# A four-layer graph network kernel: layer 3's linear score term moves from two TensorE products a block to one GpSimd add

## What is computed

```
hp = h @ lin_w.T + lin_b
u = hp @ W1.T;  v = hp @ W2.T
s = u[:, :, None, :] + v[:, None, :, :]
s = where(s > 0, s, 0.2 * s)
e = einsum('bijf,f->bij', s, a[:, 0])
e = where(adj > 0, e, -9e15)
out = elu(softmax(e) @ hp)
```

## Time and profile before

| | |
|---|---|
| median of 3 runs | 8483.6 us (8482.73 to 8487.48) |
| the profiled execution | 8497.64 us, span 8495.8 us |
| PE, DVE, ACT, POOL busy | 92%, 88%, 87%, 18% |
| mean granted clock of PE | 0.981 |
| one pass in the middle | 520 us |
| chain of work that ended last | PE 53%, DVE 16%, issue 14%, ACT 13% |

### The profile page before, as it was taken

One profiled execution on the slowest core, in us unless ns is written; L12 is line 12 of the kernel. 1 busy time (PEld: TensorE's weight loads), 2 busy tenths in 40 slices (PEclk: granted clock), 3 DMA queues, 4 the chain that ended last, 5 costly groups with the idle time before them and its releaser, 6 DMA issues.

```text
span 8495.8 us, 175156 instructions
## 1 busy us (share of the span) xinstructions
PE 7806.9 (92%) x64968; PEld 3570.9 (42%) x64968; DVE 7445.0 (88%) x10867; ACT 7388.3 (87%) x8641; POOL 1519.0 (18%) x582
## 2 busy tenths in 40 slices
PE   4889999899999999989899999999989999899998
PEld 2535344353443534435353443534435344353442
DVE  4789898898988989889898888988889898898888
ACT  3699888898888898889888888988889888898888
POOL 1212121121211112121121211212112121111000
PEclk8999999999999999999999999999999999999999
DMA  3626254362543625335253452624426254362430
GB/s 81 166 56 148 65 122 96 75 151 56 123 93 84 142 61 125 89 84 131 60 136 78 98 119 59 146 68 114 104 65 150 62 122 96 78 150 56 107 72 20
DMA packets 501426, 830.78 MB, mean 98 GB/s; under 512 B 89890, under 2 KB 155426, under 8 KB 500514
## 3 DMA queue, kind: packets, MB, share of 16 engines
q1 hardware_dynamic: 500514, 818.85, 41.5%
HBM read 76.25 MB, written 4.19 MB: 9 GB/s over the span
## 4 chain that ended last, share of the span: by engine, by line
PE 53%; DVE 16%; issue 14%; ACT 13%; SPq 2%; DMA 2%; DVEq 0%; ACTq 0%; POOL 0%; POOLq 0%
PE psum L871 23%; PE psum L784 9%; PE psum L746 7%; DVE work L1472 7%; ACT work L1130 6%; PE psum L742 4%; ACT work L994 4%; ACT work L985 3%; PE psum L765 2%; PE psum L677 2%; DVE work L1280 2%; DVE work L1308 2%; SPq L549 2%; DMA work<-work 1%; PE psum L672 1%
## 5 line engine op out<-in xcount | busy, mean ns | idle before, releaser
L1130 ACT ACTIVATE work<-v,ucol 128x1024 f32<-128x1024 f32 x3727 | 4021.4, 1141 | 318.8 <-PE psum L871 317.2
L871 PE MATMUL psum<-work,pick 128*32 128x512 f32 x32768 | 3919.9, 605 | 294.9 <-DVE top L1423 132.1
L1472 DVE TENSOR_SCALAR work<-v,ucol 128x1024 f32<-128x1024 f32 x4465 | 3379.1, 809 | 293.2 <-PE psum L871 265.7
L871 PEld LDWEIGHTS psum<-work,pick 128*32 128x32 f32 x32768 | 930.8, 110 | 2520.2 <-issue 1983.3
L1280 DVE CUSTOM_DVE_ANT_0 work<-psum,work 128x1024 f32<-128x1024 f32 x1280 | 1538.0, 1202 | 324.2 <-ACT work L985 304.4
L1308 DVE STREAM_TRANSPOSE work<-work 128x1024 f32<-128x1024 f32 x1280 | 1583.8, 1237 | 70.6 <-DMA work<-work 68.6
L994 ACT ACTIVATE work<-work,least 128x1024 f32<-128x1024 f32 x1280 | 1464.2, 1144 | 4.5 <-DVE least L1280 4.4
L985 ACT ACTIVATE work<-psum,beta 128x1024 f32<-128x1024 f32 x1024 | 1139.0, 1112 | 325.8 <-PE psum L746 267.4
L784 PEld LDWEIGHTS psum<-work,vw 128*64 128x64 f32 x16384 | 878.3, 137 | 613.8 <-issue 605.1
L784 PE MATMUL psum<-work,vw 128*64 128x128 f32 x16384 | 1119.7, 279 | 8.0 <-DMA work<-work 8.0
L742 PE MATMUL psum<-mask,ident_b 128*128 128x512 bf16 x2560 | 780.1, 387 | 236.8 <-DVE least L1280 181.5
(11 more groups left out here) (159 smaller groups left out, 5010.0 us busy)
## 6 DMA issues: line engine op xcount, KB each, us to landing
work<-work SPq DMA_DIRECT2D x2560, 256.0 KB, 4.6
adj_in<-in_adj SPq DMA_DIRECT2D x128, 512.0 KB, 4.6
tile3T<-blocks SPq DMA_DIRECT2D x512, 128.0 KB, 2.7
x_in<-in_x SPq DMA_DIRECT2D x16, 256.0 KB, 4.6
xT_both<-in_xT SPq DMA_DIRECT2D x16, 256.0 KB, 5.3
out<-yout SPq DMA_DIRECT2D x16, 256.0 KB, 2.6
work<-in_WqT SPq DMA_DIRECT2D x1, 128.0 KB
work<-in_WkT SPq DMA_DIRECT2D x1, 128.0 KB
```

Source lines behind the costliest of these rows:

```text
L871: mm = pe.matmul(score3[32 * q:32 * q + 32, cols], pick[:, 15 - kk:47 - kk], ring[u % RING][q][:, cols], start=(kk == 0), stop=(kk == 15), ...
L1130: ins = act.activation(ring[u % RING][q], v3[:], ACT.Relu, bias=ucol[:, 4 * T + q, kk:kk + 1])
L1472: ins = dve.tensor_scalar(ring[u % RING][q], v3[:], ucol[:, 4 * T + q, kk:kk + 1], 0.0, ALU.add, ALU.max)
```

## The change

The linear part is kept in `column3` in plain fp32. ACT's copy at slot 3 stays, but rounds nothing and frees the PSUM pair itself; DVE's subtraction at slot 4 is gone, and so are PE's two products in each block. Instead GpSimd writes, once a block, `column3` plus the block's mask tile into `probs3` (`mask_tile3`), and DVE's closing reduction reads `probs3` in place of the bf16 mask tile. GpSimd may do so once the block before has been transposed out of `probs3` (semaphore `s_blocks3`), that is from step 5 on; the call stands at step 6. A new semaphore, `s_mask3`, tells DVE that the sum is there; ACT waits for it too before it overwrites `column3` in the next pass.

For this GpSimd's program is rewritten to walk the slots as the other engines' do, with the conversions at slots of their own (`CONVERT_AT`) and the head adds three slots after their heads (`ADD_AT`). `convert` 4 now comes before `add_pair` 0. In slot order the new add stands: block 0 at slot 6, 1 at 22, 2 at 38, 3 at 54, 4 at 74, 5 at 102, 6 at 132, 7 at 150 (just after the deviation at slot 149 and before `convert` 6 at 152). The costs in `side_work` are changed to match, so that the split of ring units is computed anew.

```diff
-        column3 = sb("column3", [P, N], F32R)
+        column3 = sb("column3", [P, N])
...
-                if kk == (3 if T else 12):
-                    if T == 0:
-                        pe.wait_ge(freed(it3[0], ("column3", 0)), uses_before(it3[0], ("column3", 0)) + 1)
-                    for c in range(2):
-                        cols = slice(c * HALF, (c + 1) * HALF)
-                        pe.matmul(score3[:, cols], row0[:], column3[:, cols], start=False, stop=False,
-                                  skip_group_check=True)
...
-            def column_3(it):
+            def column_3(g, it):
+                if not_first(g):
+                    act.wait_ge(s_mask3, g * NT)
                 filled(act, it, ("column3", 0))
-                act.activation(column3[:], place(it, ("column3", 0)), ACT.Copy).then_inc(s_column3_hi, 1)
+                act.activation(column3[:], place(it, ("column3", 0)), ACT.Copy).then_inc(freed(it, ("column3", 0)), 1)
...
-            def top_tile3(g, T, mask):
+            def top_tile3(g, T):
                 ready(s_ring_free, ONE + g * GROUPS + (T + 1) * 16)
-                dve.tensor_tensor_reduce(probs3[:], score3, mask[:, T, :], -1.0, 3.0e38, ALU.add, ALU.min,
+                ready(s_mask3, g * NT + T + 1)
+                dve.tensor_tensor_reduce(probs3[:], score3, probs3[:], -1.0, 3.0e38, ALU.add, ALU.min,
                                          top3[:]).then_inc(s_top3, 1)
...
-            def column_3(g, it):
-                dve.wait_ge(s_column3_hi, g + 1)
-                low = column3[F:P, :]
-                dve.tensor_tensor(low, place(it, ("column3", 0))[F:P, :], low.bitcast(F32), ALU.subtract)\
-                   .then_inc(freed(it, ("column3", 0)), 1)
...
+            def mask_tile3(g, T, it):
+                if T or not_first(g):
+                    ready(s_blocks3, g * NT + T)
+                if T == 0:
+                    in_sbuf(pool, it, ("column3", 0))
+                pool.tensor_tensor(probs3[:], column3[:], mask_ring(it)[:, T, :], ALU.add).then_inc(s_mask3, 1)
...
+CONVERT_AT = {66: 0, 71: 1, 77: 2, 83: 3, 95: 4, STEPS.index(96) + 2: 5, 152: 6}
+ADD_AT = {s + 3: p for s, p in HEADS_AT.items() if p < HP - 1}
```

More of the change, by code:

```diff
@@ L235, in side_work @@
         dve += 1.25 if kk == 5 else 0.0
-        pe += {3: 0.8, 13: 1.1}.get(kk, 0.0)
+        pe += {13: 1.1}.get(kk, 0.0)
     dve += 1.4 if s in TOP3_AT else 0.0
@@ L432, in build @@
         s_q_hi = sem("s_q_hi")
-        s_column3_hi = sem("s_column3_hi")
+        s_mask3 = sem("s_mask3")
         s_relu = sem("s_relu")
@@ L1141, in layer3 @@
                     if s == 3:
[L1142 removed]
+                        column_3(g, it)
                     if kk is not None and STEPS[s] + 1 < GROUPS:
@@ L1473, in ring_units, with last_top @@
                 ins.then_inc(s_ring_dve, 1)
-            def last_top(g, it, s, tail):
+            def last_top(g, s, tail):
                 T = TOP3_AT.get(s)
                 if T:
-                    top_tile3(g, T - 1, mask_ring(it))
+                    top_tile3(g, T - 1)
                 elif T == 0 and tail:
-                    top_tile3(g - 1, NT - 1, mask_ahead(it))
+                    top_tile3(g - 1, NT - 1)
             def slots(g, it, tail, a, flagged, at):
@@ L1488, in slots @@
                         first_of(a, it, s)
-                    if g is not None and s == 4:
-                        column_3(g, it)
                     if g is not None and kk is not None:
@@ L1551, in _ @@
             layer3(B - 1, last, True, False)
-            top_tile3(B - 1, NT - 1, mask_ring(last))
+            top_tile3(B - 1, NT - 1)
             blocks_tile3(B - 1, NT - 1)
@@ L1623, in add_pair @@
                         s_accA if k == 0 else s_acc, 1)
[L1625 to L1645, removed]
@@ L1647, in _ @@
-            ahead(0, first, True)
-            ahead(1, body0, True)
-            with pool.Fori(0, B // 2 - 2) as i:
[L1650 to L1656, removed]
@@ L1657, in _, with slots @@
-            ahead(B - 1, body(B - 2, 1), False)
-            inverse_deviation(s_var3, s_rstd3, B - 1)
+            def mask_tile3(g, T, it):
[4 more added lines that the diff above has]
+                pool.tensor_tensor(probs3[:], column3[:], mask_ring(it)[:, T, :], ALU.add).then_inc(s_mask3, 1)
+            def slots(g, it, tail, a, more):
+                for s in range(SLOTS):
+                    T, kk = of_step(s)
+                    if tail and s == 20:
+                        inverse_deviation(s_var3, s_rstd3, g)
+                    if a is not None:
+                        for layer in range(2):
+                            if s == BASE[layer] + 21:
+                                inverse_deviation(s_var_a, s_rstd_a, a * 2 + layer + 1)
+                        if s == TOP_ALL_AT + 1:
+                            largest(a)
+                        if s == BASE[1] + 25:
+                            pool.wait_ge(s_xn_a, a * 4 + 4)
+                            pool.tensor_tensor(acc[:], xdup[:, :, 0, :], bp_b[:].unsqueeze(1).to_broadcast([P, NT, F]),
+                                               ALU.add).then_inc(s_acc, 1)
+                        if s in ADD_AT:
+                            add_pair(a, it, ADD_AT[s])
+                        if s == END_2 + 14:
+                            inverse_deviation(s_var2, s_rstd2, a + 1)
+                        if more and s in CONVERT_AT:
+                            convert(a, it, CONVERT_AT[s])
+                    if g is not None and kk == 6:
+                        mask_tile3(g, T, it)
+                if a is not None and more:
+                    convert(a, it, NT - 1)
@@ L1659, in _ @@
+            slots(None, first, False, 0, True)
+            slots(0, body0, False, 1, True)
+            with pool.Fori(0, B // 2 - 2) as i:
+                slots(i * 2 + 1, body(i * 2 + 1, 0), True, i * 2 + 2, True)
+                slots(i * 2 + 2, body(i * 2 + 2, 1), True, i * 2 + 3, True)
+            slots(B - 3, body(B - 3, 0), True, B - 2, True)
+            slots(B - 2, body(B - 2, 1), True, B - 1, False)
+            slots(B - 1, last, True, None, False)
             inverse_deviation(s_var3, s_rstd3, B)
```

6 lines of the change are left out of this document (2 added, 4 removed).

## The result

The changed kernel takes 8569.3 us in the median (8551.8 to 8578.1, 4 runs) against 8485.5 before (8482.7 to 8503.4): 1.0092 times as long, 95% interval 1.0070 to 1.0113. The profiled execution took 8573.8 us, span 8572.0. The forecast was 8509, slower, in a range of 8434 to 8574.

A forecast was written before the change was run, and what follows sets the result against it. PE, DVE and ACT were taken to bound it in turn, PE alone in blocks 5 and 6. +1.6 us in each of 15 passes (+24) and +1 in the last gave +25: 8522.6 us profiled, 8509 median; range 8434 to 8574.

The forecast's parts named there:

- Sign and mechanism: Whole kernel: 0.3% slower, because DVE's ring units stall under the new GpSimd adds, 136 us in all.
- block 4: Fifth block of a pass, with DVE's branch: PE's removed products gain 0.2 us, the add costs nothing.
- The loss for one add: DVE's ring units under an add: they lose 79% of its 2.5 us, 2.0 us.
- the slack: Light blocks: some 2.9 us of an early stall is absorbed if none was spent; block 1 absorbs its 2.0.
- rival 3: Whole kernel: the stalls come through in full, 5.5 us a pass and 8 in the last, 8574 us; chance 0.10.
- Block by block: Each pass, us: block 0 +0.2, block 2 +0.8, block 3 +0.5 - 0.1, blocks 5 and 6 -1.3, block 7 +1.7.
- The rule drawn from the earlier trace: Block 7: a conversion has already spent the slack, so the add's 2.0 us comes through, 1.7 after PE's gain.
- PE's pair: The two removed PE products of each block: 0.66 us of PE's time, 84 us over 128 pairs.
- The last pass: Final pass, which runs alone: three near-equal engines, +0.1 us a block, +1 in all.
- Rival 1: Whole kernel: PE bounds more, the ring absorbs the stalls; -3 us a pass, about 8434 us; chance 0.25.
- The skill's rule: DVE and GpSimd's shared ports: the loser blocks for the whole instruction, 2.5 us an add instead of 2.0.

The follow-up runs named there:

- e5_covered: e1_split_kept with the adds of blocks 0 to 3 and 7 moved under VectorE work other than ring units; 8440.9 us, ratio 0.9938.
- e1_split_kept: The changed kernel with the planner's costs of before, so ScalarE and VectorE share the ring units as before; 8558.7 us, ratio 1.0081.
- e4_slots_only: The kernel before with only GpSimd's program put into the new slot order, without the new adds; 8483.6 us, ratio 0.9992.
- e2_no_add: e1_split_kept without the GpSimd adds; the closing reduction reads the bf16 mask, layer 3's scores lack the linear part; 8430.0 us, ratio 0.9926.
- e3_pair_kept: e1_split_kept with a pair of TensorE mask products put back at the old place in each block; 8536.4 us, ratio 1.0055.
- e9_pair_block1: e1_split_kept with a pair of TensorE mask products put back in block 1 of each pass alone; 8513.3 us, ratio 1.0024.

## Why the prediction was right, and where it fell short

**Sign and mechanism held.** What makes the change slower is what DVE's ring units lose under the adds, 132 us in the traces for 136 forecast (8.0 us in each of 15 passes and 2.0 in each block of the last). With the adds under other DVE work the kernel was 118 us faster (e5_covered against e1_split_kept). Some 75 lie in the blocks whose adds moved, about 15 of them by the clock in block 1; the rest is mostly block 4 and the head, where the clock was higher. GpSimd's order costs nothing (e4_slots_only), nor does its queue (e5_covered), the planner's split nothing that can be told (e1_split_kept).

**The loss for one add** was put at 0.79 of its length, 2.0 us. Each exposed add of the last pass and of block 1 cost the units 1.9 us. The add itself was put at 2.5 us and measured 2.3. The loss per add was 1.8, 1.9, 0.9, 1.2 and 1.9 us in blocks 0, 1, 2, 3 and 7, for 2.0, 2.0, 1.2, 0.8 and 2.0 in the prediction, and nothing in 4, 5 and 6.

**The term that failed is the slack.** I took 2.9 us of slack from block 7 (4.8 us lost, 1.9 came through) and lent it to block 1, which was to absorb 2.0 and come out at 0. It came out at +1.6 (+2.7 against e2_no_add). Block 1 does have slack, but less: half an add cost 0.4 there, the whole one 1.6 where the clock stayed up and 2.9 where it fell. The sum of the loss and of the gain it eats was +1.6 a pass in the prediction and +4.4 in the traces; block 1 is 1.6 of the missing 2.8, and block 4 another 1.7 (-0.2 forecast, +1.5 found). Between passes with the same loss of clock block 4 was some 1.0 longer (96.0 and 96.9, 100.2 and 101.2), which is not explained. The other blocks give 0.5 back.

**The term that was not in the sum is the clock.** The prediction shows 0.94 for block 0 and 1.00 elsewhere and reckons with no change of it. In the traces the stall of DVE in block 1 also let PE stand idle for 2.3 us at one place in pass 7 (0.9 in e2_no_add, without the adds), and in six of 13 blocks 1 the clock then fell to 1.2 GHz, at 1.2 us a time (45.4 for 44.2). Up to 30 us of the 76 are the clock's. So the nearness to rival 3 (8574) is in part luck: rival 3 had +2.0, +1.2, +0.8 and +2.0 in blocks 1, 2, 3 and 7, where +1.6, +0.6, -0.2 and +2.0 were found, and 5.5 a pass for 4.4; block 4, the head and pass 0, of which it said nothing, brought its time near.

**Block by block otherwise** (change, forecast and found): block 0 +0.2, -0.2; block 2 +0.8, +0.6; block 3 +0.4, -0.2; blocks 5 and 6 -1.3, -1.0; block 7 +1.7, +2.0. The rule drawn from the earlier trace rows, that slack once spent is gone, held in block 7 to 0.3 us. In block 3 I gave PE's pair 0.1, and the change without its adds was worth 0.7 (46.1 to 45.4), in block 1 0.6. That this is the pair's own worth is not shown: put back beside the adds (e3_pair_kept) it cost nothing in block 3, 0.3 us in block 5 and 0.7 in block 6.

**The last pass** was put at +1 and took +7. I called its three engines near-equal and gave each block +0.1; it was +0.6, and block 1 +3.4, of which some 1.7 is the clock (0.95 there; 35.6 us at 1.00 in e3_pair_kept). There DVE has only ring units behind the transpose. These are PE's wait, and the units under the add, in block 2 of the changed kernel's last pass:

```profile
8368.74 17.86 DVE L1461 TENSOR_SCALAR work<-v,ucol 128x1024 f32<-128x1024 f32 x24
8368.89 2.56 POOL L1617 TENSOR_TENSOR probs<-column,mask 128x1024 f32<-128x1024 f32 x1 [30.52 <-DVE blocks L1425]
8372.16 0.64 PE L873 MATMUL psum<-work,pick 128*32 128x512 f32 x4 [0.98 <-DVE work L1461]
```

24 units in a row take 17.86 us where 24 x 0.66 is 15.9. PE, which before waited only for the closing reduction, runs out of ring buffers for 0.98 us; that eats more than the pair's 0.66.

**The distance.** For the profiled execution 8522.6 us were forecast and 8573.8 found, 51 more: 36 from 13 passes of 2.8, 6 from the last pass, and 9 from the head and passes 0 and 14, where clock and stops differ. Between the medians it is 60 us, as the profiled execution stood 14 us over the median that the forecast was reckoned from, and 4 over its median after.

**Rival 1** (all of it absorbed, 8434) was wrong as a forecast of this kernel, and its mechanism, a ring that absorbs the stalls, was not found. That the same edit with its adds covered takes about its time (8440.9 and 8434.7 us) is chance: there the stalls are not absorbed, they are not made.

**The skill's rule.** By "SBUF — State Buffer" ("Who interferes with whom"; the Trainium skill) the loser of the shared ports is blocked for the whole instruction. For the adds the trace is near it (1.9 us lost under 2.5). For GpSimd's 4 us `tensor_scalar`s it is not: in e5_covered one begins at 4518.44 and lasts 4.03 us; the ring unit that begins at 4518.90 takes 1.53 us for 0.75, and the next one 0.74, though the `tensor_scalar` is still running. The measurement decides: the add is the dear one, and conversions cost at their edges and in their add. The same section says that a VectorE instruction with at most one SBUF input and outside the two-port modes doesn't contend with GpSimd. The covered adds of e5_covered agree: the statistics and transposes over them kept their times (0.21 and 1.22 us each).

## What to carry to other kernels

Work given to an idle engine is not free if its instructions hold up a busy neighbour: ask what the neighbour does in those very microseconds, and pick the place by a wait on the neighbour's own progress. The same edit was 0.8% slower in one place and 0.6% faster in another, though part of both is TensorE's clock. Measure slack in the block in which it is to be spent; slack found in a like-looking block was not there, and half a stall can be absorbed where a whole one comes through.

## What the runs showed that I had not expected

A stop at DVE's branch of 2.2 to 9.7 us, mostly near 3.3, 4.8 or 9.3 us, in one pass or the next of one execution: in the kernel before, block 4 took 99 to 101 us with a long one and 94 to 97 with the others. The profile's row names ACT, and the branch stands beside it, but the long ones are passes in which TensorE's granted clock had fallen to 1.2 GHz behind an idle time of 3 us. It can move a kernel by some 20 us with no edit near it (e9_pair_block1), more than several of the terms that were summed here. Before a difference is put down to an edit, or called scatter, the granted clock of the same stretch is to be read in both kernels. What decides where in the pass the clock falls, and for how long, is open.
